# New slot orders, experts' factors made once, and the maxima's transfers issued by the scalar engine

## The reference

```
x = x + attention(layernorm(x))      # 16 heads of 8, causal softmax, out projection
x = x + experts(layernorm(x))        # 8 experts, each token goes to its best 2
expert(t) = layernorm(t + (gelu(t Wi + bi) * sigmoid(t Wg + bg)) Wo + bo) * gamma + beta
```

## Time and profile before

| | us |
|---|---|
| median of 3 runs | 1237.73 (1237.67 to 1241.8) |
| the profiled execution | 1241.94, its span 1240.2 |
| PE busy | 1105.6 |
| DVE busy | 982.0 |
| ACT busy | 796.9 |
| POOL busy | 741.8 |

### The profile page before, as it was taken

The page is one execution under the profiler, slowest core; times in us unless marked ns, Lnnn a source line. Parts: engine busy times, 40 slices in busy tenths (PEclk is TensorE's granted clock), DMA queues, the critical chain, the costliest instruction groups (busy, mean ns, idle before and its releaser), DMA issues. The chain is left out here.

```text
span 1240.2 us, 27505 instructions
## 1 busy us (share of the span) xinstructions
PE 1105.6 (89%) x8654; PEld 835.8 (67%) x8654; DVE 982.0 (79%) x2792; ACT 796.9 (64%) x1800; POOL 741.8 (60%) x1359
## 2 busy tenths in 40 slices
PE   3899999999999999999999998179999999999930
PEld 1565655665656666666666664079999999999920
DVE  4777778788788788788878873758888888888859
ACT  2465665675666666666666565268888888888810
POOL 2257475675576576576576566716666666666640
PEclk9999999999999999999999998579999999999975
DMA  5223545434434434433433421521111111111138
GB/s 145 94 77 113 168 135 166 130 93 125 130 101 125 129 109 123 131 105 113 142 112 93 138 60 36 171 53 53 52 53 54 53 53 53 53 53 53 32 123 305
DMA packets 138270, 127.38 MB, mean 103 GB/s; under 512 B 71848, under 2 KB 96432, under 8 KB 138128
## 3 DMA queue, kind: packets, MB, share of 16 engines
q1 hardware_dynamic: 127184, 103.59, 28.7%
q0 software_dynamic: 8640, 17.84, 4.4%
q10 hardware_dynamic: 2304, 4.20, 0.9%
HBM read 71.13 MB, written 54.43 MB: 101 GB/s over the span
## 5 line engine op out<-in xcount | busy, mean ns | idle before, releaser
L808 ACT ACTIVATE probs<-st 128x384 f32<-128x384 f32 (+1 forms) x768 | 389.1, 525 | 204.9 <-PE st L704 181.8
L849 DVE TENSOR_REDUCE neg_max<-sa 128x2 fp32r<-128x1024 f32 (+3 forms) x384 | 395.6, 1036 | 135.1 <-PE sa L689 126.9
L642 POOL TENSOR_SCALAR_AFFINE_SELECT probs<-probs 128x128 f32<-128x128 f32 (+1 forms) x768 | 245.5, 332 | 243.1 <-ACT probs L808 232.6
L704 PE MATMUL st<-q_stack,k_pad 128*128 128x256 f32 (+2 forms) x1024 | 338.4, 372 | 15.6 <-DMA q_stack<-max_scratch 9.1
L684 PE MATMUL sa<-k_pad,q_stack 128*128 128x256 f32 (+2 forms) x1024 | 328.1, 363 | 12.8 <-DVE neg_max L849 6.7
L684 PEld LDWEIGHTS sa<-k_pad,q_stack 128*128 128x128 f32 x1024 | 178.0, 192 | 111.8 <-issue 69.8
L704 PEld LDWEIGHTS st<-q_stack,k_pad 128*128 128x128 f32 x1024 | 177.2, 192 | 48.4 <-ACT probs L808 20.9
L1006 POOL DMA_INDIRECT y_scratch<-z,to_row x142 | 170.7, 1202 | 35.9 <-issue 35.9
L1040 PE MATMUL up<-xt_hi,w_cur 128*128 128x256 f32 x568 | 167.7, 295 | 0.0
L717 PE MATMUL pv<-probs,v_aug 128*32 128x512 f32 (+3 forms) x2048 | 167.1, 445 | 0.0
L1041 PE MATMUL up<-xt_lo,w_cur 128*128 128x256 f32 x568 | 161.6, 285 | 0.0
(11 more groups left out here) (160 smaller groups left out, 1477.2 us busy)
## 6 DMA issues: line engine op xcount, KB each, us to landing
q_stack<-q_scratch SPq DMA_DIRECT2D x64, 256.0 KB, 2.6
k_pad<-k_scratch SPq DMA_DIRECT2D x256, 64.0 KB, 2.5
xg<-rows_scratch SPq DMA_DIRECT2D x71, 130.0 KB
q_scratch<-q_hi SPq DMA_DIRECT2D x16, 512.0 KB, 3.1
k_scratch<-k_hi SPq DMA_DIRECT2D x16, 512.0 KB, 2.9
y<-y_scratch SPq DMA_DIRECT2D x16, 512.0 KB, 5.3
q_scratch<-q_lo SPq DMA_DIRECT2D x17, 256.0 KB, 3.1
k_scratch<-k_lo SPq DMA_DIRECT2D x17, 256.0 KB, 3.1
```

The costliest lines, as they stand in the source:

```text
L642: pool.affine_select(out=blk, in_=blk, compare_op=ALU.is_ge, fill=0.0, base=0, pattern=[[0, w], [1, P]], channel_multiplier=-1).then_inc(m ...
L704: last = nc.tensor.matmul(st[:, t % 2, at:at + w], k_pad[:, G * g + j, kk * P:(kk + 1) * P], q_stack[:, g, S - w:S], start=True, stop=True)
L808: nc.scalar.activation(probs[:, n % 2, j, lo:lo + w], st[:, k % 2, at:at + w], ACT.Exp).then_inc(exp_done, 1)
L849: V.tensor_reduce(neg_max[:, n % 2, heads[0]:heads[-1] + 1, i], scores[:, :, 0:(i + 1) * P], AX.X, ALU.max, negate=True).then_inc(sa_read, 1)
```

## The change

There are three edits. The strings of the four slots are new: Q, Ql, K, Kl, V, xT, zT, LG, CM and the parts of the routing stand elsewhere, in part in another slot (V in slot 1, not 0; Rc in slot 3 and one batch less behind; Rf in slot 0), while the places of A, B, PV, the maxima's tokens, OT, RC and ON among each other stay. The transfers mW and mR are issued by ACT, at the same tokens: mW behind the exponential of B4, mR behind that of B9. And gamma and beta of all experts are made once: in the order behind the slots four steps GBa to GBd, two experts each, do the selection matmul on PE into `misc` and copy it to SBUF (`gb_sb`) on ACT; the blocks read them there, and `gamma_beta` goes. The two bias matmuls of a block become one of twice the columns, with `y_ps` one tile of both halves.

```
 
 
         SLOT = {
-            0: "SR A0 B0 a0 B1 PV0 A1 B2 a1 B3 mT mE A2 B4 mW a2 B5 Rc A3 V B6 a3 B7 A4 B8 Rd PV1 PV2 PV3 a4 OT CM B9 mR AR XL A5 B10 RC a5 Re B11 ON",
-            1: "SR A0 B0 a0 Rf B1 PV0 A1 B2 out a1 B3 mT mE A2 S0 B4 mW a2 B5 A3 S1 B6 a3 B7 ln2 A4 B8 S2 PV1 PV2 PV3 a4 OT B9 mR rs2 A5 B10 RC a5 B11 ON",
-            2: "SR A0 B0 a0 ln B1 zn PV0 S3 A1 B2 a1 B3 mT mE rs1 A2 B4 mW a2 B5 zT A3 S4 B6 a3 B7 A4 LG B8 xn PV1 PV2 PV3 a4 OT B9 mR A5 B10 RC LGa a5 B11 ON",
-            3: "SR A0 Ra B0 a0 B1 PV0 S5 A1 B2 a1 B3 mT mE A2 EX S6 B4 mW a2 B5 xT A3 Rb S7 B6 a3 B7 Q A4 B8 Ql PV1 PV2 PV3 a4 OT K B9 mR A5 B10 RC a5 B11 Kl ST ON",
+            0: "SR A0 B0 a0 Rd B1 PV0 A1 B2 a1 B3 CM mT mE A2 B4 mW a2 B5 A3 B6 a3 B7 A4 B8 Re Rf PV1 PV2 PV3 a4 OT B9 mR AR XL A5 B10 RC a5 B11 ON",
+            1: "SR A0 B0 out a0 ln2 B1 PV0 S0 A1 B2 a1 B3 mT mE rs2 A2 S1 B4 mW a2 B5 V A3 S2 B6 a3 B7 A4 B8 zn PV1 PV2 PV3 a4 OT B9 mR A5 B10 RC a5 B11 ON",
+            2: "SR A0 B0 zT a0 ln B1 PV0 S3 A1 B2 a1 B3 mT mE rs1 A2 S4 B4 mW a2 B5 LG A3 B6 a3 B7 A4 B8 LGa Ra xn PV1 PV2 PV3 a4 OT B9 mR A5 B10 RC a5 B11 ON",
+            3: "SR A0 B0 EX xT a0 Rb B1 PV0 S5 A1 B2 a1 Q B3 mT mE A2 S6 B4 mW a2 Ql B5 A3 K S7 B6 a3 B7 Kl A4 B8 Rc PV1 PV2 PV3 a4 OT B9 mR ST A5 B10 RC a5 B11 ON",
         }
         AHEAD = {"SR": 4, "A": 3, "a": 3, "mT": 2, "mE": 2, "mW": 2, "mR": 2, "B": 1, "PV": 0, "OT": 0, "RC": 0, "ON": 0}
         BATCH_OF = {"ln": 2, "rs1": 2, "xn": 2, "xT": 2, "Q": 2, "Ql": 2, "K": 2, "Kl": 2, "ST": 2, "V": 1, "XL": 0,
                     "AR": -1, "out": -1, "ln2": -1, "rs2": -1, "zn": -1, "zT": -1, "LG": -1, "LGa": -1,
-                    "Ra": -1, "EX": -1, "Rb": -1, "Rc": -2, "Rd": -2, "CM": -2, "Re": -2, "Rf": -2, "S": -2}
-        FIRST = "ln rs1 xn xT Q Ql K Kl ST SR0 SR1 SR2 SR3 V"
+                    "Ra": -1, "EX": -1, "Rb": -1, "Rc": -1, "Rd": -2, "CM": -2, "Re": -2, "Rf": -2, "S": -2}
+        FIRST = "ln rs1 xn xT Q Ql K Kl ST SR0 SR1 SR2 SR3"
 
         ONCE = {-1: "WL8", 1: "SU0", 2: "SU1", 4: "SU2", 5: "SU3", 6: "WL0", 7: "WL1", 8: "WL2", 9: "WL3", 10: "WL4",
                 11: "WL5", 12: "WL6", 13: "WL7"}
 
-        LAST = """PD BU AR Rc- Rd- CM- Re- Rf- W0 W1 W2 out ln2 S0- rs2 zn S1- W3 W4 W5 W6 zT W7 W8 LG LGa S2- S3- Ra EX
+        LAST = """PD BU GBa GBb GBc GBd AR Rd- CM- Re- Rf- W0 W1 W2 out ln2 S0- rs2 zn S1- W3 W4 W5 W6 zT W7 W8 LG LGa S2- S3- Ra EX
                   S4- S5- Rb Rc Rd CM Re Rf S6- S7- RU S0 S1 S2 S3 S4 S5 S6 S7 TB W9 W10 W11 W12 W13 W14 W15"""
 
         def schedule():
@@ -236,7 +237,8 @@
                 yield kind, int(name[len(kind):] or 0), BATCHES - 1 - token.count("-")
 
         ORDER, TAIL = list(schedule()), list(tail())
-        MISC_USERS = ("xT", "Q", "K", "V", "zT", "LG", "CM", "BU")
+        GB_STEPS = ("GBa", "GBb", "GBc", "GBd")
+        MISC_USERS = ("xT", "Q", "K", "V", "zT", "LG", "CM", "BU") + GB_STEPS
         MISC_ORDER = [(kind, n) for kind, _, n in ORDER + TAIL if kind in MISC_USERS]
 
         def misc_use(kind, b):
@@ -394,7 +396,8 @@
                 before, b_ = MISC_ORDER[at - 1]
                 done, count = {"xT": (xT_done, b_ + 1), "Q": (lo_done, 2 * b_ + 1), "K": (lo_done, 2 * b_ + 2),
                                "V": (vaug_done, b_ + 1), "zT": (zT_done, b_ + 1), "LG": (logits_done, b_ + 1),
-                               "CM": (rank_done, b_ + 1), "BU": (b_up_done, 1)}[before]
+                               "CM": (rank_done, b_ + 1), "BU": (b_up_done, 1),
+                               **{step: (gb_done, i + 1) for i, step in enumerate(GB_STEPS)}}[before]
                 pe.wait_ge(done, count)
...
-                elif kind == "mW":
-                    sp.wait_ge(maxT_done, n + 1)
-                    if n >= 2:
-                        sp.wait_ge(max_landed[(n - 2) % NG], 16 * ((n - 2) // NG + 1))
-                    sp.dma_start(max_d[n % 2, :, :].rearrange("j (i q) -> (j i) q", i=NT), neg_maxT[:, n % 2, :])\
-                        .then_inc(max_stored, 16)
-                elif kind == "mR":
-                    sp.wait_ge(max_stored, 16 * (n + 1))
-                    sp.dma_start(q_stack[MROW::R, n % NG, :].bitcast(F32), max_d[n % 2, :, :])\
-                        .then_inc(max_landed[n % NG], 16)
                 elif kind == "ON":
                     b, g = n // NG, n % NG
                     sp.wait_ge(on_done, n + 1)
@@ -623,6 +617,7 @@
                         rows = b_sel[32 * c:32 * c + 32, :].rearrange("r (m q) -> r m q", q=P)
                         pool_const(pool, pool.affine_select(out=rows, in_=rows, compare_op=ALU.not_equal, fill=1.0,
                                                             base=0, pattern=[[-1, E], [0, P]], channel_multiplier=1))
+                    made["b_stack, b_sel"] = count["const"]
 
             for kind, k, n in ORDER:
                 pool_sequence(pool, kind, k, n)
...
                     pe.wait_ge(bias_loaded, 16 * 11)
                     nc.tensor.transpose(misc[:, 0:2 * E * FC], b_rows[:, :], ident[0:2 * E * FC, 0:2 * E * FC])\
                         .then_inc(misc_written, 1)
+                elif kind in GB_STEPS:
+                    misc_free(pe, kind, n)
+                    pe.wait_ge(r_const, made["b_stack, b_sel"])
+                    for half in range(2):
+                        e = 2 * GB_STEPS.index(kind) + half
+                        last = nc.tensor.matmul(misc[:, half * 2 * D:(half + 1) * 2 * D], b_sel[:, e * P:(e + 1) * P],
+                                                b_stack[:, D:3 * D], start=True, stop=True)
+                    last.then_inc(misc_written, 1)
 
         @block.scalar
         def _(act):
@@ -807,10 +810,25 @@
                     lo, w, at = ((0, 512, 0), (512, 384, 0), (896, 384, 128))[third]
                     nc.scalar.activation(probs[:, n % 2, j, lo:lo + w], st[:, k % 2, at:at + w],
                                          ACT.Exp).then_inc(exp_done, 1)
+                elif kind == "mW":
+                    act.wait_ge(maxT_done, n + 1)
+                    if n >= 2:
+                        act.wait_ge(max_landed[(n - 2) % NG], 16 * ((n - 2) // NG + 1))
+                    act.dma_start(max_d[n % 2, :, :].rearrange("j (i q) -> (j i) q", i=NT), neg_maxT[:, n % 2, :])\
+                        .then_inc(max_stored, 16)
+                elif kind == "mR":
+                    act.wait_ge(max_stored, 16 * (n + 1))
+                    act.dma_start(q_stack[MROW::R, n % NG, :].bitcast(F32), max_d[n % 2, :, :])\
+                        .then_inc(max_landed[n % NG], 16)
 
             for kind, k, n in TAIL:
                 act_sequence(act, kind, k, n)
-                if kind == "W":
+                if kind in GB_STEPS:
+                    i = GB_STEPS.index(kind)
+                    act.wait_ge(misc_written, misc_use(kind, n))
+                    act.wait_ge(pv_written, GROUPS_ALL)
+                    nc.scalar.activation(gb_sb[:, i * 4 * D:(i + 1) * 4 * D], misc[:, :], ACT.Copy).then_inc(gb_done, 1)
+                elif kind == "W":
                     e, m = k // 2, k % 2
                     act.wait_ge(ffn_loaded, 16 * 2 * E)
                     act.wait_ge(pv_written, GROUPS_ALL)
...
@@ -931,16 +949,15 @@
         z = sb("z", [P, NR, 2, D])
 
         up = pb("up", [P, 4, F])
-        y_ps = [pb(f"y_ps{h}", [P, D]) for h in range(2)]
+        y_ps = pb("y_ps", [P, 2, D])
         xt_ps = pb("xt_ps", [P, BR])
-        gb_ps = misc[:, 0:2 * D]
 
         gathered = [sem(f"gathered{u}") for u in range(NX)]
         scattered = [sem(f"scattered{u}") for u in range(NR)]
         xt_written, xhi_done, xlo_done = sem("xt_written"), sem("xhi_done"), sem("xlo_done")
         wi_copied, wg_copied = sem("wi_copied"), sem("wg_copied")
         up_written, up_read = sem("up_written"), sem("up_read")
-        hid_done, gb_written = sem("hid_done"), sem("gb_written")
+        hid_done = sem("hid_done")
...
@@ -1047,23 +1064,16 @@
                 pe.wait_ge(hid_done, 2 * s + 2)
                 if not before(s, 1):
                     pe.wait_ge(res_done, s)
+                nc.tensor.matmul(y_ps[:, :, :], b_sel[:, bass.ds(e * P, P)],
+                                 b_stack[:, 0:D].unsqueeze(1).broadcast_to([P, 2, D]), start=True, stop=True)
                 for h in range(2):
-                    nc.tensor.matmul(y_ps[h][:, :], b_sel[:, bass.ds(e * P, P)], b_stack[:, 0:D],
-                                     start=True, stop=False)
                     for c in range(FC):
-                        last = nc.tensor.matmul(y_ps[h][:, :], hid[:, u % 2, c, h * P:(h + 1) * P],
+                        last = nc.tensor.matmul(y_ps[:, h, :], hid[:, u % 2, c, h * P:(h + 1) * P],
                                                 wo_sb[:, bass.ds(e * (FC * D) + c * D, D)],
-                                                start=False, stop=(c == FC - 1))
```

(23 more changed lines are left out.)

## The result

The changed kernel takes 1298.7 us (median of 4 runs, 1293.54 to 1300.88) against 1237.7 (4 runs, 1237.27 to 1241.8): a ratio of 1.0483, 95% interval 1.0455 to 1.0512. The forecast was 1275 in a range of 1238 to 1308; the result lies inside this range, above the 1255 to 1295 that had a chance of 0.48. The profiled execution took 1300.88, its span is 1299.0.

What follows compares the result with a forecast made beforehand. TensorE (PE) was taken as the bound in attention and experts. Against the profiled 1241.94 us, +16 +5 +31 -3 -11 -1 = +37 gave 1279, or 1275 with the runs' median 4.2 lower; range 1238 to 1308.

Steps and rivals of the forecast that it cites:

- K's wait: New slot 3: K waits about 1.4 us for Ql; with side effects 2.2 us in 14 slots, +31.
- experts: Expert blocks: gamma/beta matmul gone (0.10) and one bias matmul gone (0.05), in 71 blocks, -11.
- load and store on ACT, the old waits taken off: Attention slots: maxima's load +16, with 14 us of present waits taken off, and store +5.
- other moves, last slots: V, routing, ln2 and ln moved: together -3; normalisation of batch 14 leaves a slot without A steps: -1.
- the signs that I had named: B0 waits 0.4 to 0.6 us, K about 1.4 once a batch; expert blocks 5.05; attention 45 to 50 longer.
- Maxima's load on ACT: Slot end: load leaves as B9's exponential starts, B0 0.48 late in 63 slots: 30 us, less 14: +16.
- Maxima's store: Between the exponentials of B4 and B5: delays B7 by 0.35 us in 16 bare slots, +5.
- rival A: Clock falls after each K wait, about 1.5 us a slot: +21, 1296 us; chance 0.15.
- B: ACT issues the maxima's load only after B9's exponential ends: +31, 1306 us; chance 0.1.
- C: ACT issues the maxima's load before B9's exponential, while that waits for PE: -30, 1245 us; chance 0.12.
- D: DVE's reductions pace the slot, so K's and mR's waits fall into time PE loses anyway: 1213 us; chance 0.1.
- E: Scalar queue as late as SP's, orders worth nothing; only the experts' 11 us: 1227 us; chance 0.05.

Runs made afterwards that it cites:

- e2: Kernel before, with only the maxima's store and load (mW, mR) issued by ACT, same places in the orders: 1282.63 us, 1.0362.
- e4: Changed kernel with K and Kl back in their old places and ST behind Kl as it was: 1270.56 us, 1.0260 to the kernel before.
- e3: Kernel before, with only the four new slot orders and what belongs to them; maxima on SP, experts unchanged: 1257.54 us, 1.0151.
- e1: Kernel before, with only the experts' part (gamma and beta made once, bias matmuls merged); orders and queue as before: 1222.23 us, 0.9880.
- e12: e1 with one token moved: in slot 0 the loads SR stand behind the maxima's store, not at the slot's start: 1215.70 us, 0.9810 to the kernel before.
- e5: Kernel before, with only the maxima's load (mR) issued by ACT; the store stays on SP: 1271.40 us, 1.0268.
- e9: e10 with V in slot 1 as well, ahead of A3: 1233.42 us, 0.9950 to the kernel before.
- e7: Changed kernel with ln2 behind A1's reduction in slot 1, not ahead of it: 1296.72 us, 1.0467 to the kernel before.
- e10: e1 with slot 3 alone changed: xT and Q early, K behind B7, Kl behind B8, ST behind mR: 1233.97 us, 0.9963 to the kernel before.
- e11: Kernel before, with only the two bias matmuls of an expert block merged; gamma and beta made in every block: 1231.54 us, 0.9945.
- e8: Changed kernel with mW, mR on SP, Q, Ql, K, Kl, ST in their old places, ln2 as in e7: 1244.24 us, 1.0055 to the kernel before.

## Why the prediction was right, and where it was not

Slower was right, and both mechanisms on which it rested are there. That the range held has some luck in it: K's wait and the experts, each some 4 us lower than forecast, made up for 7 of the 30 us by which the rest was too small. The sizes compare so (measured from the ratios, times 1238):

| step | forecast | measured |
|---|---|---|
| load and store on ACT, the old waits taken off | +21 | +44.8 (e2) |
| K's wait for Ql | +31 | +27.6 (e4) |
| other moves, last slots | -4 | about +2: -9 (e3 less K) and the 11 that e2 has taken off too |
| experts | -11 | -14.9 (e1) |
| sum | +37 | +59.8 |

Of the signs that I had named, the waits of B0 and K came as described; the expert block is 4.99 in place of 5.05 us, and attention is 75.6 us longer in the records, not 45 to 50.

**Maxima's load on ACT.** The mechanism is as written: the load leaves with B9's exponential and every B0 waits. What was mis-sized is the wait. From B9's second matmul to B0 the four slots take 9.56 us after and 7.20 in e3: 2.36 a batch, or 0.59 for each B0, in place of 0.48. And B0 to B1 takes 0.67 where B0 has waited and 0.56 where not, 0.4 a batch, for which I had nothing. So it is 2.8 by 15 batches, 41, for my 30. The 14 us of present waits were rightly taken off against the kernel before: in e12, which has next to none, the same stretch is 0.95 a batch shorter than before (6.82 for 7.77). On the old orders the sum closes: e5 against e12 is 3.2 a batch, 48, less the 14, and e5 measured +33.2 for my +16.

My issue to B0 of 1.86 is 1.95, 1.94 and 2.01 in the mean after slots 0 to 2 (1.81 at the least), and 2.35 after slot 3 (2.29 in e2; one case is 389.47 to 391.72): there the DMA engines are busy with the stores of q or k, issued 1.4 to 2.2 us ahead, until 1.0 to 1.3 us after the load's issue. In e4, where the stores were issued some 3 us ahead and the DMA engines fall idle 0.1 us after the load's issue, it is 1.92 after slot 3 (393.88 to 395.74 is one).

**Maxima's store.** +5 forecast, 11.6 on the old orders (e2 against e5). In the changed kernel against e3, from B1 to B9, it is 0.15 us in slot 0, for which I had 0.35, 0.4 in slot 1 and nothing in slots 2 and 3: LG and K ahead of B6 cover it there as forecast. V in slot 1 does not: there the maxima are late behind ln2, and ACT waits for them at the store (1.89 us before 429.20, above). Together 0.57 a batch, 9 us.

**K.** Right by its steps: the weight load idle 1.35 us for the 1.4 forecast, in the forecast place. The clock did not fall behind it: 1.00 over 400 to 700, so rival A is out for waits of that length. What fell was the clock behind the 4.56 us wait of group 6, to 0.52 over 7 us; the earlier trace rows had shown the same after a shorter pause.

**The other moves.** Small as a sum, but not by my reasons. Within it two larger things cancel: slot 0 gets shorter by 1.6, 0.9 of it where V stood and 0.5 in the waits, since ST is early (I had written that its effect is covered by mR's waits, which holds only with mR on ACT); slot 1 gets longer by 1.0, of which e9 gives V 0.2 and e7 leaves most to ln2's work ahead of the reductions, a move that I had seen and put into -3. (ln in slot 2, which I named beside it, stood ahead of A1's reduction before the change too.) The early xT and Q, for which I gave 0.5 us as lost cover, are part of what made slot 3 of e10 1.2 us longer. The one long wait behind the selection matrix, 5.7 us here and 7.4 in e3, I did not see.

**Experts.** The gamma and beta matmul is right at 0.11 for 0.10; the bias' 0.05 is 0.11, since I gave the break behind a bias to one of the two, and the merged one has none. The tail's rounds cost 0, as forecast (e1 and e11); a round takes 1.1 to 1.3 us for my estimate of 1.1.

**The rivals.** B (issue after the exponential's end) and C (issue while it waits for PE) are both out: the issue stands at 433.51, the exponential at 433.50. C was the result of what the Trainium skill says in Perfetto Trace Analysis, section Per-engine timelines, that the sequencer is free once an instruction is in the wait queue. The trace agrees only in part. Where ACT was still busy with a copy, e2 shows

```profile
389.23 0.60 ACT L774 ACTIVATE k_hi<-misc 128x512 fp32r<-128x512 f32 x1 [2.39 <-PE misc L736]
389.47 0.50 ACTq L808 DMA_DIRECT2D q_stack<-max_scratch  x1
389.72 0.87 ACT L798 ACTIVATE probs<-st 128x384 f32<-128x384 f32 x2
```

The load's issue (389.47) stands behind the exponential in program order and begins 0.25 us before it runs, but 0.04 after B9's matmuls end (389.15 + 0.28 in the records). It is so in all 13 batches after slot 3 in e2, and in the other slots the issue comes 0.04 after B9's matmuls too. So a transfer overtakes an exponential that waits for the engine, and not one that waits for its semaphore. D (the reductions absorb the waits) is out by e2 and e4: both waits were worth their full length. E is out by e2.

## What to carry to other kernels

A transfer that another engine's chain needs should stand in its issuing engine's order ahead of every instruction that becomes ready later than the transfer does; one place in that order was worth 24 us here. The issues themselves are not free either where the engine has other work: the store between the exponentials cost 11.6. Before a transfer is moved to another queue to free it, read what stands ahead of it in its own: the waits of the kernel before came from five loads, and the wait ahead of them, in front of one small store, and moving them behind it was the only change of the old orders that made the kernel faster. And when parts are measured alone, look for a gain that two of them make: it can be had only once.

## What the runs showed of the hardware

- On ACT the load's issue begins when the wait of the exponential ahead of it is met, 0.25 us before that exponential runs where the engine is busy (389.47 against 389.72). Its issue takes 0.50 us for the load of four rows and 0.31 for the store, as on SP (0.52 and 0.30 to 0.36), and the exponential behind a store starts about 0.35 after it (428.85, 429.20).
- From issue to B0 the load takes 1.94 to 2.01 us in the mean of a slot, on ACT (after) as on SP (1.94 in e8, slot 0), and 2.35 where stores of 512 and 256 KB were issued 1.8 and 1.4 us ahead of it.
- With a wait of 1.35 us for K in each batch the granted clock was 1.00 over 400 to 700; after a wait of 4.56 us it was 0.52 for 7 us.
- Behind a store of 8 KB that SP issued right after five loads, the load that waits for it left 2.04 us later in the mean (1.59 to 3.64, e1, slot 0).
- A bf16 bias matmul of 128 columns takes 0.06 and delays the fp32 matmul behind it by 0.053; one of 256 columns takes 0.12 and delays it by nothing.
